# A macaron block on one core: the attention stage's engine programs in a new order

## The reference

```python
x = x + 0.5 * ffn(layernorm(x))
x = x + attn(layernorm(x))
x = x + 0.5 * ffn(layernorm(x))

# attn: 16 heads of 32
q, k = exp(split_heads(x @ Wq.T + bq)), exp(split_heads(x @ Wk.T + bk))
v = split_heads(x @ Wv.T + bv)
kv = cumsum(k[..., :, None] * v[..., None, :], axis=1)      # running state
num = einsum('zsD,zsDd->zsd', q, kv)
den = sum(q * cumsum(k, axis=1), -1, keepdims=True)
out = merge_heads(num / den) @ Wo.T + bo

# ffn: 32 experts, each takes its 8 best tokens of a sequence
probs = softmax(x @ gate_w.T + gate_b, over tokens)
vals, idx = top_k(probs, 8)
merged = sum_k vals * x[idx]                   # one row per (sequence, expert)
o = gelu([merged, 1] @ w1) ; o = [o, 1] @ w2
out = zeros.at[idx].add(o * vals)
```

## Time and profile before

| | |
|---|---|
| Median of 3 runs | 2498.9 us (2496.84 to 2501.86) |
| The profiled execution's own time | 2500.54 us |
| Its span in the profile | 2498.80 us |
| TensorE busy | 2090.8 us, 84% |
| VectorE busy | 839.2 us, 34% |
| ScalarE busy | 765.8 us, 31% |
| GpSimd busy | 590.3 us, 24% |
| DMA | 762.21 MB, mean 305 GB/s |

### The profile page before, as it was taken

How to read it: one execution, slowest core, us unless ns; L and a number is a source line. 1 busy time by engine, 2 the same in 40 slices (tenths; PEclk the granted TensorE clock), 3 DMA queues, 4 the chain that set the end, 5 groups by cost and what they waited for, 6 DMA issues and landing times.

```text
span 2498.8 us, 44463 instructions
## 1 busy us (share of the span) xinstructions
PE 2090.8 (84%) x18836; PEld 1228.0 (49%) x18836; DVE 839.2 (34%) x1656; ACT 765.8 (31%) x1321; POOL 590.3 (24%) x691
## 2 busy tenths in 40 slices
PE   6979999999999999888888888888866666666665
PEld 3436656566665666566666666666631111111111
DVE  6831111111111111567777777776720000000002
ACT  6831111111111111456665656556520000000000
POOL 2210000000000000366666666666612000000002
PEclk9989999999999999999999999999987888888888
DMA  9759999999999999364443444444289999999995
GB/s 357 306 215 376 406 400 412 412 404 401 409 409 404 410 392 368 102 220 132 148 133 128 144 131 146 131 135 132 84 322 422 424 424 425 425 425 423 424 425 214
DMA packets 130660, 762.21 MB, mean 305 GB/s; under 512 B 21108, under 2 KB 21108, under 8 KB 77216
## 3 DMA queue, kind: packets, MB, share of 16 engines
q1 hardware_dynamic: 118688, 701.35, 71.6%
q10 hardware_dynamic: 9216, 50.34, 4.8%
q0 software_dynamic: 2560, 7.70, 0.8%
HBM read 648.09 MB, written 105.91 MB: 302 GB/s over the span
## 4 chain that ended last, share of the span: by engine, by line
PE 47%; DMA 33%; DVE 6%; POOL 4%; ACT 4%; issue 3%; SPq 1%; POOLq 0%; ACTq 0%; DVEq 0%
PE ps L266 44%; DMA big<-in_L_ffn_w 31%; DVE big L274 2%; PE ps L270 2%; SPq L18 1%; POOL s L1215 1%; DVE big L1187 1%; POOL s L1241 1%; DMA big<-in_L_attn_x 1%; POOL big L1224 1%; DMA out_x<-big 1%; ACT big L1115 1%; POOL big L1218 1%; ACT big L1086 1%; DVE big L1147 1%
## 5 line engine op out<-in xcount | busy, mean ns | idle before, releaser
L266 PE MATMUL ps<-big 128*32 128x512 f32 (+6 forms) x13904 | 1073.4, 428 | 289.1 <-DMA big<-in_L_ffn_w 208.6
L266 PEld LDWEIGHTS ps<-big 128*32 128x32 f32 (+3 forms) x13904 | 405.1, 128 | 875.2 <-issue 534.1
L274 DVE TENSOR_TENSOR big<-ps,big 128x512 f32<-128x512 f32 (+1 forms) x565 | 340.2, 649 | 147.6 <-PE ps L266 108.4
L266 PE MATMUL ps<-wth,xth 128*128 128x512 f32 x768 | 308.9, 402 | 3.0 <-ACT big L805 3.0
L266 PE MATMUL ps<-wth,xtl 128*128 128x512 f32 x768 | 299.6, 390 | 0.0
L266 PE MATMUL ps<-wtl,xth 128*128 128x512 f32 x768 | 299.0, 389 | 0.0
L682 ACT ACTIVATE big<-ps 128x512 f32<-128x512 f32 x64 | 38.3, 598 | 804.3 <-PE ps L266 804.3
L1212 POOL TENSOR_TENSOR big<-big 128x1 f32<-128x1 f32 x64 | 35.3, 551 | 926.8 <-ACT big L1065 876.3
L266 PE MATMUL ps<-wo,s 128*128 128x512 f32 x768 | 212.4, 430 | 1.4 <-ACT s L1118 1.4
L706 DVE COPY big<-ps 128x128 f32<-128x128 f32 x64 | 18.3, 286 | 580.9 <-PE ps L640 580.9
L814 DVE TENSOR_SCALAR big<-ps,big 128x512 f32<-128x512 f32 x64 | 48.0, 751 | 402.5 <-PE ps L266 402.5
(11 more groups left out here) (111 smaller groups left out, 1802.3 us busy)
## 6 DMA issues: line engine op xcount, KB each, us to landing
big<-in_L_ffn_w SPq DMA_DIRECT2D x256, 2048.0 KB, 22.5
p_scratch<-big ACTq DMA_DIRECT2D x64, 768.0 KB, 10.1
big<-p_scratch SPq DMA_DIRECT2D x64, 768.0 KB, 4.5
big<-in_L_attn_x SPq DMA_DIRECT2D x16, 1024.0 KB, 13.1
xt_scratch<-big SPq DMA_DIRECT2D x16, 1024.0 KB, 11.4
big<-xt_scratch SPq DMA_DIRECT2D x16, 1024.0 KB, 16.6
big<-in_L_attn_x SPq DMA_DIRECT2D x64, 256.0 KB, 2.9
x_weight_scratch<-big SPq DMA_DIRECT2D x64, 256.0 KB, 3.2
```

What stands on the lines that cost most here:

```text
L266: return nc.tensor.matmul(o, l, r, start=start, stop=stop, skip_group_check=True)
L274: return nc.vector.tensor_tensor(o, p, q, op)
```

## The change

The attention functions of TensorE, ScalarE, VectorE and GpSimd are written anew; SyncE's is not touched, nor is any other stage.

- TensorE: in an iteration the order is now scores of n; FFN transposes of n-2; the low part of the projection of n-1; key-value products of n; the rounded half of the prefix sums of n+1; logits; merges; the other half of the prefix sums; state and values of n; correction of n+2; key transposes of n+1; rest-of-sum of n+1; query transposes of n+1; the high part of the projection of n.
- The merges use bank 1 (the queries' and the FFN transposes') in place of bank 3; `bank1` holds the waits for it. They stand in iterations 4, 6 and 7 of a batch.
- VectorE: one mask instruction over banks 4 to 7; one add for query and value and one for the key; no bn_stats, bn_aggr and eps add. The correction of tile n+2 is drained at the end of iteration n (before: that of n+1 at its start). The residual sum `X1` also gives its row sum. Top-k's steps are spread: maximum in iteration 1 of a batch, replacement and mask in 2, weights in 3.
- ScalarE: a square with accumulation of `X1` for its variance; both squares write their elements (which nobody reads) into a PSUM bank, 7 or 0. Query exponential first, then key; the value's scaling is moved back; the key copy `KT` is that of n+1, at the end.
- GpSimd: eps and scale for the new square; the order of the steps.

```diff
@@ attention_pe
-                if live and c < 7:
-                    pe.wait_ge(s_pr, n + 1)
-                    mm(ps[:, 2, :], AFTER, KH, False, False)
-                    mm(ps[:, 2, :], AFTER, KL, False, False).then_inc(s_after, 1)
-                if live:
-                    pe.wait_ge(s_ke, n + 1)
-                    pe.wait_ge(s_x2, n - 1)
-                    transpose4(0, PB[i][:, 1, :]).then_inc(s_ktT, 1)
-                    pe.wait_ge(s_qn, n + 1)
-                    transpose4(1, PB[i][:, 0, :]).then_inc(s_qtT, 1)
...
                 if live:
                     pe.wait_ge(s_kt, n + 1)
                     pe.wait_ge(s_qt, n + 1)
-                    for s_ in (s_x1, s_tk, s_tq, s_tv):
+                    pe.wait_ge(s_st, n)
+                    for s_ in (s_x1sq, s_tk, s_tqv):
                         pe.wait_ge(s_, min(n + 2, NT))
...
+                if 0 <= n - 2 < NT:
+                    pe.wait_ge(s_x2n, n - 1)
+                    bank1(n - 1)
+                    transpose4(1, XN3[(n - 2) % NX]).then_inc(s_g3T, 1)
                 if 0 <= n - 1 < NT:
-                    pe.wait_ge(s_ath, n)
-                    for g in range(4):
-                        mm(ps[:, 0, :], h4(ATH)[:, g, :], WOH[:, g, :], g == 0, False)
-                        mm(ps[:, 0, :], h4(ATH)[:, g, :], WOL[:, g, :], False, False)
                     pe.wait_ge(s_atl, n)
                     for g in range(4):
                         t = mm(ps[:, 0, :], h4(ATL)[:, g, :], WOH[:, g, :], False, g == 3)
                     t.then_inc(s_op, 1)
...
+                m = n + 1
+                if 0 <= m < NT:
+                    pe.wait_ge(s_ke, m + 1)
+                    pe.wait_ge(s_x2sq, m - 1)
+                    transpose4(0, PB[m % 4][:, 1, :]).then_inc(s_ktT, 1)
+                    if m % 8 < 7:
+                        pe.wait_ge(s_pr, m + 1)
+                        mm(ps[:, 2, :], AFTER, KH, False, False)
+                        mm(ps[:, 2, :], AFTER, KL, False, False).then_inc(s_after, 1)
+                    pe.wait_ge(s_qn, m + 1)
+                    pe.wait_ge(s_xt3, n - 1)
+                    bank1(n)
+                    transpose4(1, PB[m % 4][:, 0, :]).then_inc(s_qtT, 1)
+                if live:
+                    pe.wait_ge(s_kt, min(n + 2, NT))
+                    pe.wait_ge(s_x2sq, n)
+                    pe.wait_ge(s_ath, n + 1)
+                    for g in range(4):
+                        mm(ps[:, 0, :], h4(ATH)[:, g, :], WOH[:, g, :], g == 0, False)
+                        mm(ps[:, 0, :], h4(ATH)[:, g, :], WOL[:, g, :], False, False)
@@ attention_act
+                if nxt:
+                    act.wait_ge(s_x1, m + 1)
+                    act.wait_ge(s_x1ve, m - 1)
+                    nc.scalar.activation(ps[:, 7, :], X1[m % 4], ACT.Square, bias=SX1[m % 2], scale=-float(D),
+                                         accum_out=SQ1[m % 2]).then_inc(s_x1sq, 1)
...
+                if nxt:
+                    act.wait_ge(s_ktT, m + 1)
+                    act.wait_ge(s_S, 4 * m)
+                    nc.scalar.copy(KT, ps[:, 0, :]).then_inc(s_kt, 1)
@@ attention_dve
+                if live:
+                    dve.wait_ge(s_S, 4 * n + 4)
+                    dve.wait_ge(s_av, n)
+                    tt(MASKED, SCORES, TRI.unsqueeze(1).broadcast_to([128, 16, 128]), ALU.mult).then_inc(s_st, 1)
...
-                    for r in range(4):
-                        dve.wait_ge(s_S, 4 * n + r + 1)
-                        tt(h4(ST[:, r, :]), h4(ps[:, 4 + r, :]), TRI.unsqueeze(1).broadcast_to([128, 4, 128]),
-                           ALU.mult).then_inc(s_st, 1)
...
+                if n >= 10 and c == 2:
+                    topk_replace(dve, 8 + (n - 10) // 8)
+                if n >= 15 and c == 7:
+                    merge_end_dve(dve, 8 + (n - 15) // 8, 1)
+                if n >= 11 and c == 3:
+                    topk_weights(dve, 8 + (n - 11) // 8)
+                m = n + 2
+                if m < NT:
+                    dve.wait_ge(s_c, m + 1)
+                    dve.wait_ge(d_x1[m % 4], 16 * (m // 4 + 1))
+                    dve.wait_ge(s_x1sq, m - 1)
+                    nc.vector.scalar_tensor_tensor(out=X1[m % 4], in0=ps[:, 7, :], scalar=0.5, in1=X1[m % 4],
+                                                   op0=ALU.mult, op1=ALU.add,
+                                                   accum_out=SX1[m % 2]).then_inc(s_x1, 1)
+                    dve.wait_ge(d_pb[m % 4], 16 * (m // 4 + 1))
+                    tt(PB[m % 4][:, 0::2, :], ps[:, 4:7:2, :], PB[m % 4][:, 0::2, :], ALU.add).then_inc(s_tqv, 1)
+                    tt(PB[m % 4][:, 1, :], ps[:, 5, :], PB[m % 4][:, 1, :], ALU.add).then_inc(s_tk, 1)
+                if n >= 10 and c == 2:
+                    topk_mask(dve, 8 + (n - 10) // 8)
+                if n >= 9 and c == 1:
+                    topk_max(dve, 8 + (n - 9) // 8)
@@ attention_pool
+                    pool.wait_ge(s_x1sq, m + 1)
+                    nc.gpsimd.tensor_scalar(VE[m % 2], SQ1[m % 2], 1.0 / D ** 3, EPS, ALU.mult,
+                                            ALU.add).then_inc(s_x1ve, 1)
```

More of the change, by code:

```diff
@@ L179, in macaron_block @@
         IDX = nc.alloc_sbuf_tensor_at("idx", [128, 16], mybir.dt.uint32, offset=base + 4 * (sm_at + 160))[:, :]
+        SX1 = [SM[:, 6 + 8 * i:7 + 8 * i] for i in range(2)]
+        SQ1 = [SM[:, 22 + 8 * i:23 + 8 * i] for i in range(2)]
         NG = NT // 4
@@ L246, in kvs, with groups, steps @@
             return 7 * (n // 8) + min(n % 8, 7)
-        def logged(m):
-            return m // 4 * 4
+        def groups(k):
+            return max(0, min((k - 1) // 4, NT // 4))
+        def steps(k, first):
+            return 8 + max(0, min((k - first) // 8 + 1, B))
         def quad(b):
@@ L995, in attention_pe @@
                     t.then_inc(s_op, 1)
-                if nxt:
+                if live and c < 7:
+                    pe.wait_ge(s_v, n + 1)
+                    pe.wait_ge(s_at, n)
+                    for g in range(4):
+                        for r in range(4):
+                            at_ = 128 * g + 32 * r
+                            t = mm(ps[32 * r:32 * r + 32, 3, 32 * g:32 * g + 32], PB[i][:, 1, at_:at_ + 32],
+                                   PB[i][:, 2, at_:at_ + 32], True, True)
+                    t.then_inc(s_kv, 1)
+                if 0 <= n + 1 < NT:
                     pe.wait_ge(s_pr, n + 1)
@@ L1010, in attention_pe @@
                     if live:
-                        pe.wait_ge(s_st, 4 * n + 4)
+                        pe.wait_ge(s_st, n + 1)
+                    for s_ in (s_x1sq, s_tk, s_tqv):
+                        pe.wait_ge(s_, n + 2)
                     b = m // 8
@@ L1040, in attention_pe @@
                 if n == -2:
                     outer_pe(pe, 5)
-                if 0 <= n - 2 < NT and (n - 2) % 4 == 3:
-                    pe.wait_ge(s_xt3, n - 1)
-                    for k in range(4):
-                        for j in range(4):
-                            t = mm(ps[32 * j:32 * j + 32, 1, 0:128], GT[:, k, :], XT3[j][:, k, :], k == 0, k == 3)
-                    t.then_inc(s_lg3, 1)
-                if n >= 10 and done == 2:
-                    pe.wait_ge(s_at, min(n + 1, NT))
-                    merge_transpose_pe(pe, 8 + gb, 3)
@@ L1065, in attention_act @@
             nc.scalar.activation(BK, BK, ACT.Exp).then_inc(s_eb, 1)
-            for n in range(-2, NT + 9):
+            for n in range(-2, NT + 8):
                 live = 0 <= n < NT
                 nxt = 0 <= n + 1 < NT
-                m = n + 1
-                gb, done = divmod(n - 10, 8)
+                m, c = n + 1, n % 8
+                if nxt:
[3 more added lines that the diff above has]
+                                         accum_out=SQ1[m % 2]).then_inc(s_x1sq, 1)
                 if live:
-                    act.wait_ge(s_ktT, n + 1)
-                    act.wait_ge(s_S, 4 * n)
-                    nc.scalar.copy(KT, ps[:, 0, :]).then_inc(s_kt, 1)
                     act.wait_ge(s_qtT, n + 1)
```

262 lines of the change are left out of this document (117 added, 145 removed).

## The result

| | before | changed |
|---|---|---|
| Median | 2499.1 us (2496.8 to 2501.9, 4 runs) | 2423.0 us (2417.7 to 2426.1, 4 runs) |
| Ratio | 1 | 0.9693 (95% interval 0.9671 to 0.9714) |
| Profiled execution, span | 2500.54, 2498.80 | 2426.14, 2424.40 |
| Forecast | | 2409, range 2388 to 2456 |

The change wins 76 us; 90 were forecast. In the changed kernel the matmul helper is L272, the transpose helper L276 and VectorE's tensor-tensor helper L280 (L266, L270 and L274 before). Cut by the same marks as the earlier trace rows (first, eighth and last score block), the changed kernel's stretches are these; I add the stretch ahead and the one behind. Behind start, end and length a row has the busy time of TensorE's matmuls, its weight loads (PEld), VectorE, ScalarE and GpSimd, each with the number of instructions, then the granted clock of TensorE, the DMA share and GB/s.

The account below looks back on a forecast made before the run. No engine was full; the loop was tied by waits, and its gain carried to the end. Mask and state add would set a regular tile. Gains of 84.7 and 5.5 made 90.2: 2410.3, median 2409 us, range 2388 to 2456.

Parts of the forecast that it names:

- The seven batches: Attention loop after the first batch: 86.3 us a batch against 98.4, a gain of 84.7 us.
- The start: First batch of the attention loop: a gain of 5.5 us, with scores 4 to 7 taking 31.9 instead of 35.4.
- chunks that are issued earlier: First batch: prefetched weight chunks issued about 2 us earlier, so the 15.73 us store wait ends as much earlier.
- the prologue: Ahead of the attention loop: keeps its chain, a change of 0.
- a logits tile: Tile with gate logits: blocks 3.51 + 0.87 = 4.38, plus 6.57, makes 10.95 us.
- The last tile of a batch: Tile without key-value products, put at 9.69 us.
- Tile 6: Tile with merged tokens, 1.76 us extra, put at 11.84 us.
- The three limits: Per tile: mask plus state add (forecast, 0.52), in-order ScalarE loop (rival, 0.27), TensorE alone (rival, 0.08).
- the ScalarE loop: Correction to GpSimd's difference: 0 to 0.6 us of slack; as binding rival, 11.2 a tile, 2447 us, chance 0.27.
- My allowance of 0.1 a tile: Added to the 85.5 us batch sum for what could not be placed, giving 86.3 us.
- The cover: Projection's high part, 1.91 us before the next scores, covers two ScalarE copies; VectorE's drain lies under 3.44 us.
- The collision I weighed: Top-k weights against GpSimd's query scaling: VectorE waits 0.7; if VectorE came first, TensorE waits 1.3, 9 us in all.

Follow-up runs that it names:

- e1: The changed kernel run again with nothing edited: 2425.5 us, ratio 0.9684 to the kernel before.
- e8: Changed kernel with the residual sum's variance again made by bn_stats, bn_aggr and an add on VectorE, without the ScalarE square: 2448.6 us, ratio 0.9780.
- e5: Changed kernel with the projection's high part moved back ahead of its low part in the next iteration: 2493.7 us, ratio 0.9950.
- e7: Changed kernel with the one mask instruction of 2048 elements made four of 512 again: 2425.9 us, ratio 0.9691.
- e3: Changed kernel with key-value products right behind the scores on TensorE and the state add ahead of the mask on VectorE: 2428.4 us.
- e4: Changed kernel with the normalised row written twice, 0.85 us more of ScalarE's time per tile: 2435.9 us.
- e6: Changed kernel with top-k's maximum, replacement and mask together in iteration 2 of a batch: 2442.6 us, ratio 0.9754.
- e12: Changed kernel with the three weight chunks loaded in iterations 1, 9 and 17 and top-k's weights behind the correction's drain on VectorE: 2411.6 us, ratio 0.9647.
- e11: Changed kernel with prefix sums together, weight chunks in iterations 1, 9 and 17, and key-value products right behind the scores on TensorE alone: 2428.4 us, ratio 0.9700.

## Why the prediction was right

**The direction, the mechanism and the regime held.** 90.2 us were forecast and 76 measured. On the profiled executions it is 74.4. The seven batches gave 78.7 (forecast 84.7), the stretch from the first to the eighth score block 3.3 (5.5), the time to the first score block -6.3 (0), and the end -1.3 (0).

**The start gave nothing, where 5.5 were forecast.** The scores 4 to 7 took 32.0 us (31.9 forecast), so the 3.5 of that term came. The other 2, for chunks that are issued earlier, did not: from score block 0 to 4 it is 47.85 us, before 47.77. Of the -6.3, about 4 stand ahead of the attention stage and are variation or a cost that one trace of the kernel before can't tell from it (e1). Some 2 are the prologue, which I set at nothing: from the last ScalarE copy of the stage ahead to the first score block it is 14.06 us, 13.66 in e1, and 11.82 before. Of the 2.2 us 1.7 can be read on ScalarE: with the square in between, the first exponential starts 3.76 us behind the table load, before 2.71, and the rounded half of the key comes another 0.6 later, since the query's exponential now goes first. But taking the square out gave nothing back. In e8, which has bn_stats in its place, the exponential starts after 2.72 us, and the first score block still comes 13.62 us after that copy: bn_stats stands there ahead of VectorE's adds for the next tile, and the block waits 1.22 us for them:

```profile
1038.65 1.56 PE L272 MATMUL ps<-big 32*128 32x128 f32 x64 [1.22 <-DVE big L280]
```

No run has bn_stats behind the adds, as the kernel before has it, so what the prologue could win is open.

**The step that was short is TensorE's own time.** I summed the blocks of the earlier trace rows as if their lengths did not depend on their neighbours: 10.95 for a logits tile. The rows after give 11.34 without an idle moment: projection 1.11 + 2.03 in place of 2.87, prefix sums 0.44 + 0.43 for 0.46, logits 1.01 for 0.87, and 0.3 won back on the three lone transposes and 0.08 on the products. Tiles 1, 4 and 5 are short by 0.39, 0.24 and 0.39 for this, 1.0 us a batch of the 1.7 between 85.5 and 87.15. e5 shows the price of the cut projection alone (2.93 against 3.14).

**Two tiles were summed wrongly, and the slips cancel.** The last tile of a batch stands at 9.69. By the prediction's own terms it is 10.22: blocks of 3.51 less the products 0.46, plus the merge's closing transposes 0.6, plus 6.57; the mask alone would hold it to 10.15. It measured 10.16. Tile 6 stands at 11.84, but the rest-of-sum of the tile after it, the last of its batch, does not exist, so the terms give 11.27. It measured 12.19. Some 0.4 of the difference are the neighbours again. The rest is a wait that the prediction did not have: without the rest-of-sum between the key and the query transposes TensorE reaches the high part before ScalarE has copied the key, and the eight transposes take 1.33 us up to the high part, where in tile 4 the two blocks take 0.79:

```profile
1469.33 1.09 PE L276 MATMUL ps<-big 128*128 128x128 f32 x8
1470.66 2.11 PE L272 MATMUL ps<-wo,s 128*128 128x512 f32 x8 [0.24 <-ACT big L1148]
```

One slip is 0.53 too short and the other 0.57 too long; that the sum of the batch did not suffer is luck.

**The three limits were named, but not where each holds.** I placed the mask and state add as the bound of a regular tile (10.46; measured 10.32) and the ScalarE loop 0 to 0.6 us behind it. e7 shows that the mask's length counts in tiles 0, 2 and 3 (e3, which puts the mask later, lengthens the same three), and e4 gives ScalarE's loop 0.17 us of slack in tile 2 and none in tile 7. In tiles 1, 4 and 5 TensorE never waits, and 0.85 us more on ScalarE move nothing; tile 6, with its short wait, doesn't move by that either. e8 shows the limit of this: VectorE's drain of the correction, 1 us later, makes these four 0.6 longer. My allowance of 0.1 a tile covered half of the error.

**The cover was right and its beneficiary wrong.** e5 gives back 66 of 76 us. The high part hides VectorE's drain first; I had weighed the ScalarE copies as what it covers. The parts don't add up to the whole: e5, e8 and e6 give back 66, 24 and 17 us, each with the other parts in place.

**Top-k and the clock.** Spreading top-k is worth about 17 us (e6); no slow projection is left in the batches, and the clock row says 1.00.

**The collision I weighed came, on its other side.** I took the row (VectorE waits, 2.03 us in the earlier trace rows) over the case that GpSimd waits. The trace after has the weights 0.07 to 0.13 us ahead of the query scaling in all seven batches, GpSimd held up (up to 2.12 for 1.05) and a wait of TensorE behind it. The Trainium skill ("SBUF — State Buffer", Who interferes with whom) has it that a VectorE instruction with two SBUF inputs contends with a GpSimd instruction that reads SBUF, and that the order of issue decides who blocks. The rows agree down to 0.07 us; closer than that the starts don't tell, since before, in two of seven batches, VectorE started 0.02 us ahead and was still the one held up (2.14 us). e12, which keeps the two apart, takes 0.44 us off that tile.

## What to carry to other kernels

When engines are balanced, place a tile by hand for each loop and each kind of tile, and ask which loop binds in which tile: here one edit could act on three tiles of eight, another on four. Work of the bound engine that waits for nothing belongs between what it hands to the other engines and the block that needs their answer, even at the price of cutting a block in two; then look for the wait which the cut hides before joining it again. Write the blocks of every kind of tile out in the new order before adding them up: a block that is missing in one tile also takes its cover away. Take the length of a TensorE block from a row with the same neighbours.

## What the runs showed of the hardware

- What a matmul block costs up to the next one depends on its neighbours: 12 projection matmuls 2.93 us, 8 and 4 of them apart 3.14; the same 4 take 1.10 with key-value products behind them and 1.01 with prefix sums (e3, e11); two prefix-sum matmuls 0.46 together, 0.87 with logits between.
- With TensorE idle for 2.46 to 2.60 us once a batch (e6), the granted clock was at 0.50 behind it in four of seven batches.
- The same square of 128x512 took 722 ns written to SBUF and 690 to 697 written to PSUM. The Trainium skill ("ScalarE: Activation LUTs", Step-by-step: what each stage is for) says that PSUM is the faster destination for ScalarE; the rows agree, with 4%.
- The mask, one VectorE instruction of 2048 elements, took 2.292 us; four of 512 made the three tiles where it counts 0.11 to 0.14 us longer (e7) and the others not at all.
